# Two attention stages in a six-stage kernel: retention's scores six slots later, and softmax scores made twice

## The chip, the cores and the metric

The kernel runs on one core of one Trainium2 chip. The metric is the device time of one execution in microseconds (us); lower is better. A core has a matrix engine (TensorE, PE in the profile), three engines for element-wise work (VectorE or DVE, ScalarE or ACT, GpSimd or POOL), an engine that only issues transfers here (SyncE, SP) and 16 DMA engines. Each engine runs its own instructions in order; semaphores tie them together. TensorE writes to PSUM, which has eight banks of 512 float32 columns; the others work from SBUF or PSUM.

## What is computed

Sixteen sequences x of 256 tokens and 128 channels go through two layers, each a feed-forward net, an attention and another net. Two attentions matter here, both with 16 heads of 8 channels. The first is retention, with no softmax:

```python
qkv = x @ w_qkv.T                       # q, k are rotated and scaled, position by position
scores = jnp.einsum('bhtd,bhsd->bhts', q, k) * HEAD_DIM ** (-0.5)
scores = scores * mask[None]            # causal, decaying
y = jnp.einsum('bhts,bhsd->bhtd', scores, v)    # then group norm, gate, projection
```

The second is plain attention:

```python
q = q * scale
attn = jax.nn.softmax(jnp.einsum('bnhd,bmhd->bhnm', q, k), axis=-1)
out = jnp.einsum('bhnm,bmhd->bnhd', attn, v)
return out.reshape(B, N, C) @ w_proj.T + b_proj
```

## The kernel before

`program` runs six stages one after the other on an x that stays in SBUF: routed net, `retention`, routed net, `relative_ffn` (attention with relative positions and a mixture), `plain_attention`, `relative_ffn`. The change touches the second and the fifth.

In both a batch is one sequence. Its q and k are made in float32, split into three bfloat16 parts whose sum is the float32 value (`parts`), written by SP to DRAM in six combinations (`write_slots` in retention, `stack_parts` in the other: six DMAs, 768 KB) and read back as `qs` and `ks` (two DMAs of 384 KB), where a head's combinations lie on 48 partitions (the tiles have 96, the rest zero). So one bfloat16 matmul over 96 rows gives scores of nearly float32 precision. The loads of batch i overwrite those of batch i-2, so SP waits for the scores of that batch.

Retention is written as slots. A step has NS = 16 slots n; `at(s, n, slot)` gives the batch i for which slot number `slot`, counted from the start of its own first step, falls on slot n of step s, or None. Each engine goes through steps and slots and issues whatever is due, so the numbers set the order on each engine. For batch i: x is normalised and turned (slot 6), q and k projected (9, 11), v (13), the gate g (15); the parts are made in slots 17 to 21; scores of group r (four heads) and half follow at 36 + 4r + 2half, masks one slot later on DVE, the copies of the other block on ACT (`later`), values at 42 + 4r; then statistics (56), group means on PE (58, 62), 64 to 69 the scale, shift and gate, 72 the output projection, 74 the addition to x. Scores go to three banks (`sd`) and one (`so`), y to two, and all small products share two banks (`desk`, a `Bench`), taken in the order of the list `order`: an item waits until the one two places before it has been taken away.

Plain attention runs `softmax_attention` with `rel` false. In each step of 16 iterations n, PE makes the scores of two heads and one half of the queries (`scores`, 128 queries x 256 keys, twice; four banks `sr`), DVE takes their maximum over the keys (`maxima`, L1849), ACT the exponential with that maximum as bias and the sum as a by-product (`exponentials`, L1718: 32 of 256 columns a batch, each with a read of the accumulator), PE transposes the result in four blocks (`turn_round`, L1586: 64 a batch), ACT and DVE copy the blocks to SBUF in turn (`take_turned`, L1698 and L1688: 8 each), and PE multiplies them with the values (`values`, L1599). The sums are inverted, spread and transposed, and multiply y. Three steps overlap: projections of batch s, parts of s-1, attention of s-2, the end of s-3.

## Time and profile before

| | us |
|---|---|
| time, median of 3 runs (range) | 3241.97 (3240.16 to 3244.74) |
| the profiled execution | 3240.78 |
| its span, first to last instruction | 3239.0 |
| PE / PE weight loads busy | 2893.4 / 2344.7 |
| DVE / ACT / POOL busy | 2067.5 / 1993.3 / 1996.2 |
| retention | about 320 to 580 |
| plain attention | about 1883 to 2238 |

A matmul's duration includes the latency of its end, and an ACT duration overlaps with that of the one before it, so in this kernel the distance from start to start tells what an instruction costs its engine. A row that ends in x4 is four instructions merged. The granted clock is a share of TensorE's full speed of 2.4 GHz; half is 1.2 GHz. A bracket at the end of a row is the time in which the engine was idle before it, and what ended that.

### The profile page before, as it was taken

The page shows a single profiled execution, that of the slowest core. Times are in us where ns is not written, and L with a number is a line of the kernel's source. Part 1 is how long each engine was busy: PE and PEld are TensorE (multiplying, and loading weights), DVE is VectorE, ACT ScalarE, POOL GpSimd, SP SyncE. Part 2 cuts the span into 40 slices and gives each one's busy share as a digit, 9 for nine tenths or more (in the row PEclk, how much of TensorE's full clock was granted, in tenths as well). Part 3 has the DMA queues.
Part 4 walks back from the last instruction along what each step waited for, and adds up shares of the span by engine and source line. Part 5 has one row for each costly group of instructions (what it writes and reads, how often), then busy time and mean ns, then how long its engine had stood idle before and what let it go on. Part 6 is the DMA issues. An engine that isn't in the chain of part 4 may idle for free. (4 is left out here: it accounts for less than half of the span.)

```text
span 3239.0 us, 64162 instructions
## 1 busy us (share of the span) xinstructions
PE 2893.4 (89%) x21536; PEld 2344.7 (72%) x21536; DVE 2067.5 (64%) x4642; ACT 1993.3 (62%) x5893; POOL 1996.2 (62%) x2415
## 2 busy tenths in 40 slices
PE   6999677699969999997999979896999999979998
PEld 4788555488857877785788856664777778858886
DVE  5444466454458888885555558885788888745554
ACT  2232333223258988985444459996899889844443
POOL 4223554322268878874999932222788778669997
PEclk8999889899979999998999989998999999989999
DMA  3000445000022212212545533332122112145544
GB/s 106 1 1 1 110 109 111 1 1 1 1 48 56 45 40 45 55 41 107 193 186 195 186 88 79 79 79 49 41 49 52 41 41 58 23 177 190 193 186 170
DMA packets 145535, 261.88 MB, mean 81 GB/s; under 512 B 13402, under 2 KB 118106, under 8 KB 122298
## 3 DMA queue, kind: packets, MB, share of 16 engines
q1 hardware_dynamic: 145210, 257.78, 27.3%
q8 instruction: 176, 2.88, 0.4%
q14 instruction: 149, 1.22, 0.1%
HBM read 204.06 MB, written 53.67 MB: 80 GB/s over the span
## 5 line engine op out<-in xcount | busy, mean ns | idle before, releaser
L2252 POOL TENSOR_TENSOR f6m_ht_lo<-f6m_ht,f6m_ht_hi 128x512 fp32r<-128x512 f32 x256 | 331.1, 1311 | 32.3 <-ACT f6m_ht_hi L2197 23.3
L2252 POOL TENSOR_TENSOR f4m_ht_lo<-f4m_ht,f4m_ht_hi 128x512 fp32r<-128x512 f32 x256 | 331.9, 1316 | 30.4 <-ACT f4m_ht_hi L2197 22.2
L2232 DVE SCALAR_TENSOR_TENSOR f4m_ht<-f4m_hr,f4m_gate 128x512 f32<-128x512 f32 x256 | 176.4, 691 | 167.4 <-PE f4m_hr L2128 159.3
L2232 DVE SCALAR_TENSOR_TENSOR f6m_ht<-f6m_hr,f6m_gate 128x512 f32<-128x512 f32 x256 | 176.3, 691 | 167.1 <-PE f6m_hr L2128 160.5
L2197 ACT ACTIVATE f6m_ht_hi<-f6m_ht 128x512 fp32r<-128x512 f32 x256 | 161.9, 634 | 190.6 <-DVE f6m_ht L2232 190.5
L2197 ACT ACTIVATE f4m_ht_hi<-f4m_ht 128x512 fp32r<-128x512 f32 x256 | 161.9, 634 | 189.9 <-DVE f4m_ht L2232 189.6
L1718 ACT ACTIVATE f6a_pr<-f6a_sr,f6a_nm 128x256 f32<-128x256 f32 x512 | 241.4, 487 | 47.9 <-DVE f6a_nm L1849 47.8
L1718 ACT ACTIVATE f4a_pr<-f4a_sr,f4a_nm 128x256 f32<-128x256 f32 x512 | 241.2, 487 | 47.9 <-DVE f4a_nm L1849 47.9
L1718 ACT ACTIVATE a_pr<-a_sr,a_nm 128x256 f32<-128x256 f32 x512 | 257.9, 585 | 11.2 <-DVE a_nm L1849 11.1
L1980 POOL TENSOR_TENSOR f4a_rr<-f4a_tmp 128x256 f32<-128x256 f32 x256 | 187.7, 733 | 101.9 <-DVE f4a_tmp L1857 100.0
L1980 POOL TENSOR_TENSOR f6a_rr<-f6a_tmp 128x256 f32<-128x256 f32 x256 | 187.5, 732 | 101.7 <-DVE f6a_tmp L1857 99.6
L1857 DVE TENSOR_TENSOR f4a_tmp<-f4a_ur,f4a_turn 128x512 f32<-128x512 f32 x256 | 174.9, 683 | 76.7 <-PE f4a_ur L1558 73.2
L1857 DVE TENSOR_TENSOR f6a_tmp<-f6a_ur,f6a_turn 128x512 f32<-128x512 f32 x256 | 174.9, 684 | 76.1 <-PE f6a_ur L1558 72.6
L1849 DVE TENSOR_REDUCE a_nm<-a_sr 128x2 f32<-128x512 f32 x256 | 173.4, 684 | 57.5 <-PE a_sr L1570 57.5
L1849 DVE TENSOR_REDUCE f4a_nm<-f4a_sr 128x2 f32<-128x512 f32 x256 | 175.9, 687 | 41.4 <-PE f4a_sr L1576 41.1
L1849 DVE TENSOR_REDUCE f6a_nm<-f6a_sr 128x2 f32<-128x512 f32 x256 | 175.8, 687 | 41.4 <-PE f6a_sr L1576 41.0
L1986 POOL TENSOR_TENSOR f6a_rr_lo<-f6a_rr,f6a_rr_hi 128x256 fp32r<-128x256 f32 x256 | 190.6, 745 | 0.9 <-ACT f6a_rr_hi L1792 0.9
L1986 POOL TENSOR_TENSOR f4a_rr_lo<-f4a_rr,f4a_rr_hi 128x256 fp32r<-128x256 f32 x256 | 190.2, 743 | 0.9 <-ACT f4a_rr_hi L1792 0.9
L1574 PE MATMUL f6a_sr<-f6a_pe_hi,f6a_rr_hi 128*128 128x256 f32 x512 | 187.3, 366 | 0.0
L1574 PE MATMUL f4a_sr<-f4a_pe_hi,f4a_rr_hi 128*128 128x256 f32 x512 | 187.3, 366 | 0.0
L1586 PE MATMUL a_tr<-all_table,a_pr 128*128 128x128 f32 x1024 | 157.4, 276 | 5.8 <-ACT a_pts L1698 3.4
L1718 ACT ACTIVATION_READ_ACCUMULATOR a_pr<-a_sr,a_nm 128x1 f32 x512 | 162.3, 317 | 0.0
(420 smaller groups left out, 9783.9 us busy)
## 6 DMA issues: line engine op xcount, KB each, us to landing
f4m_gate<-f4m_gates SPq DMA_DIRECT2D x64, 1024.0 KB, 4.6
f6m_gate<-f6m_gates SPq DMA_DIRECT2D x64, 1024.0 KB, 4.6
r_scratch<-r_parts SPq DMA_DIRECT2D x32, 192.0 KB, 2.2
all_qs<-r_scratch SPq DMA_DIRECT2D x16, 384.0 KB, 4.8
all_ks<-r_scratch SPq DMA_DIRECT2D x16, 384.0 KB, 6.7
f4a_scratch<-f4a_parts SPq DMA_DIRECT2D x32, 192.0 KB, 2.2
all_qs<-f4a_scratch SPq DMA_DIRECT2D x16, 384.0 KB, 5.2
all_ks<-f4a_scratch SPq DMA_DIRECT2D x16, 384.0 KB, 6.6
```

The costliest lines, as they stand in the source:

```text
L1574: nc.tensor.matmul(out, rr_hi[at], pe_hi[:, :], start=False, stop=False)
L1586: mm = nc.tensor.transpose(ring.bank(b, n // 2)[:, o:o + P], pr[:, n % 4, x, st * P:(st + 1) * P], k.ident)
L1718: last = nc.scalar.activation(pr[:, n % 4, x, :], sr.bank(b, n)[:, x * T:(x + 1) * T], ACT.Exp, bias=nm[:, n % SB, x:x + 1], accum_out=zs[ ...
L1849: nc.vector.tensor_reduce(nm[:, n % SB, :], sr.bank(b, n).rearrange("p (x s) -> p x s", x=2), AX.X, ALU.max, negate=True).then_inc(nm_read ...
L1857: nc.vector.tensor_tensor(tmp[:, hs % 2, :, :], ur.bank(b, hs).rearrange("p (u t) -> p u t", u=2), turn[:, :, :], ALU.mult).then_inc(ur.em ...
L1980: nc.gpsimd.tensor_tensor(rr[:, hs % RAW, :], tmp[:, hs % 2, 0, :], tmp[:, hs % 2, 1, :], ALU.add)\
L1986: nc.gpsimd.tensor_tensor(rr_lo[:, hs % RRS, :], rr[:, hs % RAW, :], rr_hi[:, hs % RRS, :], ALU.subtract)\
L2197: nc.scalar.activation(ht_hi[:, n % RB, :], ht[:, n % RB, :], ACT.Copy).then_inc(hi_ready, 1)
L2232: nc.vector.scalar_tensor_tensor(ht[:, n % RB, :], hr[:, n % HB, :], 0.0, gate[:, q % GB, n % LOADED, :], ALU.max, ALU.mult).then_inc(ht_r ...
L2252: nc.gpsimd.tensor_tensor(ht_lo[:, n % RB, :], ht[:, n % RB, :], ht_hi[:, n % RB, :], ALU.subtract)\
```

## The change

In retention all slots from the scores on are six higher (scores 42 + 4r + 2half, values 48 + 4r, statistics 62, and so on to 80), the stage has one more step, and the desk's order is another: gm, gv, xt, q, k, v, o, g instead of xt, o, q, gm, k, v, gv, g.

Plain attention gets a function of its own, in the manner of retention. The scores are made twice. First by queries, as before, in two banks instead of four; only DVE reads them, for the maxima. POOL splits the negated maxima of a half of the heads into three bfloat16 parts (`split_maxima`, six operations), PE transposes them (slots 43 and 51), ACT copies 24 rows to `mrow` and SP copies those to rows 96 to 119 of that batch's `qs` (`move`: 24 rows to eight heads). Rows 96 to 119 of the keys hold a one where a row belongs to the head (`pick_rows`, once). Then PE makes the scores by keys over 120 rows (`turned`, slots 50 to 65, three banks), which gives the transposed scores less the maximum; ACT takes the exponential of 512 columns straight into `pts`, without bias or sum; values follow at 56 + 4r. Columns of ones in the values' tile give the sums in the same product; y goes to all 512 columns of its bank, is transposed (71), divided on DVE (`divide`, 72), transposed back (74) and projected (77). The normalisation of x moves from DVE to POOL, one cast of q and k from DVE to ACT. There are three buffers for qs and ks instead of two, and four for the values instead of two, both cleared at the start of the stage.

```diff
+KROWS = ROWS + 3 * H // 2
...
-    LAST = B + 3
+    LAST = B + 4
...
-            order += [(name, s - lag) for name, lag in (("xt", 0), ("o", 4), ("q", 0), ("gm", 3), ("k", 0), ("v", 0), ("gv", 3),
+            order += [(name, s - lag) for name, lag in (("gm", 4), ("gv", 4), ("xt", 0), ("q", 0), ("k", 0), ("v", 0), ("o", 4),
...
-                i = at(s, n, 4 * NS + 8)
+                i = at(s, n, 4 * NS + 14)
...
-                i = at(s, n, 3 * NS + 10)
+                i = at(s, n, 4 * NS)
...
-                i = at(s, n, 3 * NS + 14)
+                i = at(s, n, 4 * NS + 4)
...
-                            i = at(s, n, 36 + 4 * r + 2 * half)
+                            i = at(s, n, 42 + 4 * r + 2 * half)
...
-                        i = at(s, n, 42 + 4 * r)
+                        i = at(s, n, 48 + 4 * r)
...
-    softmax_attention(nc, tag, x_sb, k, io)
...
+    NS, NB, VB, SB, PB = 16, 3, 4, 2, 3
+    SCORES, TURNED = 2 * NS, 3 * NS + 2
+    HALF = H // 2
+    TOP = 3 * HALF
+    MOVED = 16
...
+            order += [(name, s - lag) for name, lag in (("m1", 3), ("xt", 0), ("v", 0), ("yt", 4), ("qk", 0), ("yb", 4), ("m0", 2),
+                                                       ("o", 4)) if 0 <= s - lag < B]
...
+            def move(i, half):
+
+                desk.done(sp, f"m{half}", i)
+                if i:
+                    sp.wait_ge(moved[half], i * MOVED)
+                sp.dma_start(queries(i)[ROWS:KROWS, half * HALF:(half + 1) * HALF, :],
+                             mrow[0:TOP, half, :].unsqueeze(1).to_broadcast([TOP, HALF, T])).then_inc(moved[half], 16)
+
+            for s in range(B + 3):
+                if 0 <= s - 3 < B:
+                    move(s - 3, 1)
+                if 0 <= s - 2 < B:
+                    move(s - 2, 0)
+                if s < B:
+                    if s >= 1:
+                        sp.wait_ge(stacked, s * LANDED)
+                    sp.wait_ge(parts_ready, s + 1)
+                    write_slots(sp, parts[:, s % 2], scratch[s % 2], bounced)
+                    if s == 2:
+                        sp.wait_ge(third_clear, 4)
+                    if s >= NB:
+                        sp.wait_ge(st_filled, (s - NB + 1) * NS)
+                    sp.wait_ge(bounced, (s + 1) * BOUNCED)
+                    for u, dst in enumerate((queries(s), keys(s))):
+                        sp.dma_start(dst[0:USED, :, :].rearrange("s h t -> s (h t)"),
+                                     scratch[s % 2, u].rearrange("n (d h) t -> (n d) (h t)", h=H)).then_inc(stacked, 16)
...
+            def scores(i, n):
+                r, jj, t = n // QUAD, n // 2 % 2, n % 2
+                g = i * NS + n
+                if n == 0:
+                    pe.wait_ge(stacked, (i + 1) * LANDED)
+                if g >= SB:
+                    pe.wait_ge(nm_ready, g - SB + 1)
+                for x in range(2):
+                    h = QUAD * r + 2 * jj + x
+                    mm = nc.tensor.matmul(sr[:, g % SB, x * T:(x + 1) * T], queries(i)[0:ROWS, h, t * P:(t + 1) * P],
+                                          keys(i)[0:ROWS, h, :], start=True, stop=True)
+                mm.then_inc(sr_filled, 1)
+
+            def turned(i, m):
+                r, jj, t = m // QUAD, m // 2 % 2, m % 2
+                g = i * NS + m
+                if g == 0:
+                    pe.wait_ge(ones_set, 6)
+                if m % (NS // 2) == 0:
+                    pe.wait_ge(moved[m * 2 // NS], (i + 1) * MOVED)
+                if g >= PB:
+                    pe.wait_ge(pr_ready, g - PB + 1)
+                for x in range(2):
+                    h = QUAD * r + 2 * jj + x
+                    mm = nc.tensor.matmul(st[:, g % PB, x * T:(x + 1) * T], keys(i)[0:KROWS, h, t * P:(t + 1) * P],
+                                          queries(i)[0:KROWS, h, :], start=True, stop=True)
+                mm.then_inc(st_filled, 1)
+
+            def values(i, r):
+                if r == 0:
+                    desk.done(pe, "v", i)
+                    if i:
+                        pe.wait_ge(y_copied, i)
+                pe.wait_ge(pr_ready, i * NS + (r + 1) * QUAD)
+                for t in range(TT):
+                    for j in range(QUAD):
+                        q = slice(j * QUAD * HD, (j + 1) * QUAD * HD)
+                        mm = nc.tensor.matmul(y_ps[q, r // 2 * T:(r // 2 + 1) * T], vm[:, i % VB, t, r, q], pts[:, r % 2, t, j, :],
+                                              start=(r == 0 and t == 0), stop=(r == QUAD - 1 and t == TT - 1),
+                                              skip_group_check=True)
+                mm.then_inc(av_done, 1)
...
+                for half in range(2):
+                    i = at(s, n, SCORES + 11 + half * 8)
+                    if i is not None:
+                        name = f"m{half}"
+                        pe.wait_ge(split, (2 * i + half) * 6 + 6)
+                        desk.free(pe, name, i)
+                        for t in range(TT):
+                            mm = nc.tensor.transpose(desk.bank(name, i)[:, t * P:(t + 1) * P], mf[:, half, t, :], k.ident)
+                        mm.then_inc(desk.filled, 1)
...
+                i = at(s, n, 4)
...
+                i = at(s, n, 6)
...
+                i = at(s, n, TURNED + 21)
...
+                i = at(s, n, 8)
...
+                i = at(s, n, TURNED + 24)
...
+                i = at(s, n, TURNED + 27)
...
+            pe.wait_ge(k.loaded, k.loaded_count)
+            for s in range(LAST + 1):
+                for n in range(NS):
+                    i = batch(s, 2)
+                    if i is not None:
+                        scores(i, n)
+                    project(s, n)
+                    for m in range(NS):
+                        i = at(s, n, TURNED + m)
+                        if i is not None:
+                            turned(i, m)
+                    for r in range(QUAD):
+                        i = at(s, n, TURNED + 6 + 4 * r)
+                        if i is not None:
+                            values(i, r)
...
+            def exponentials(i, m):
+                r, jj, t = m // QUAD, m // 2 % 2, m % 2
+                g, R = i * NS + m, i * QUAD + r
+                act.wait_ge(st_filled, g + 1)
+                if m % QUAD == 0 and R >= 2:
+                    act.wait_ge(av_done, R - 1)
+                nc.scalar.activation(pts[:, r % 2, t, 2 * jj:2 * jj + 2, :].rearrange("p x t -> p (x t)"), st[:, g % PB, :],
+                                     ACT.Exp).then_inc(pr_ready, 1)
...
+            def pick_rows():
+
+                act.wait_ge(loaded, LOADS)
+                for n, tile in enumerate((k.ks[ROWS:KROWS, 0, :, :], k.ks[ROWS:KROWS, 1, :, :], k3[ROWS:KROWS, :, :])):
+                    for half in range(2):
+                        copy(tile[:, half * HALF:(half + 1) * HALF, :],
+                             pick[ROWS:KROWS, :].unsqueeze(2).to_broadcast([TOP, HALF, T])).then_inc(ones_set, 1)
...
+                    copy(parts[:, i % 2, 0, :, :], desk.bank("qk", i).rearrange("p (u t) -> p u t", u=2))
+                    copy(qk[:, :, :].rearrange("p u t -> p (u t)"), desk.bank("qk", i)).then_inc(desk_taken, 1)
+                    if i == 1:
+                        pick_rows()
...
+            def maxima(i, n):
+                r, jj, t = n // QUAD, n // 2 % 2, n % 2
+                g, q = i * NS + n, 2 * i + r // 2
+                dve.wait_ge(sr_filled, g + 1)
+                if n % (NS // 2) == 0 and q >= 2:
+                    dve.wait_ge(split, (q - 2) * 6 + 3)
+                at_ = r % 2 * QUAD + 2 * jj
+                nc.vector.tensor_reduce(nm[:, r // 2, t, at_:at_ + 2], sr[:, g % SB, :].rearrange("p (x s) -> p x s", x=2), AX.X,
+                                        ALU.max, negate=True).then_inc(nm_ready, 1)
...
+            def divide(i):
+                desk.full(dve, "yt", i)
+                if i:
+                    desk.full(dve, "yb", i - 1)
+                bank = desk.bank("yt", i).rearrange("p (h g c) -> p h g c", h=2, c=QUAD * HD)
+                for hf in range(2):
+                    last = nc.vector.reciprocal(rz[:, hf, :, :], bank[:, hf, :, 16 * (1 - hf):16 * (1 - hf) + 2])
+                last.then_inc(rz_ready, 1)
+                dve.wait_ge(rz_ready, i + 1)
+                for hf in range(2):
+                    last = nc.vector.tensor_tensor(
+                        yn[:, :, :].rearrange("p t (j c) -> p (t j) c", c=QUAD * HD)[:, :, 16 * hf:16 * hf + 16]
+                        .rearrange("p g (r d) -> p g r d", d=HD),
+                        bank[:, hf, :, 16 * hf:16 * hf + 16].rearrange("p g (r d) -> p g r d", d=HD),
+                        rz[:, hf, :, :].unsqueeze(3).to_broadcast([P, 2 * QUAD, 2, HD]), ALU.mult)
+                last.then_inc(yn_ready, 1)
...
+            def clear_third():
+                for tile in (q3, k3):
+                    for rows in (slice(32, 64), slice(64, ROWS)):
+                        nc.vector.memset(tile[rows, :, :].rearrange("p s t -> p (s t)").bitcast(F32), 0.0).then_inc(third_clear, 1)
...
+                    nc.vector.tensor_copy(parts[:, i % 2, 1, :, :], rest[:, :, :]).then_inc(part1, 1)
+                    if i == 1:
+                        clear_third()
...
+            def split_maxima(i, half):
+
+                q = 2 * i + half
+                pool.wait_ge(nm_ready, i * NS + (half + 1) * (NS // 2))
+                if i:
+                    desk.full(pool, f"m{half}", i - 1)
+                whole = nm[:, half, :, :]
+                first, second, third = (mf[:, half, :, n * HALF:(n + 1) * HALF] for n in range(3))
+                nc.gpsimd.tensor_copy(b1[:, :, :], whole).then_inc(split, 1)
+                pool.wait_ge(split, q * 6 + 1)
+                nc.gpsimd.tensor_tensor(r1[:, :, :], whole, b1[:, :, :], ALU.subtract).then_inc(split, 1)
+                pool.wait_ge(split, q * 6 + 2)
+                nc.gpsimd.tensor_tensor(first, whole, r1[:, :, :], ALU.subtract).then_inc(split, 1)
+                nc.gpsimd.tensor_copy(b2[:, :, :], r1[:, :, :]).then_inc(split, 1)
+                pool.wait_ge(split, q * 6 + 4)
+                nc.gpsimd.tensor_tensor(third, r1[:, :, :], b2[:, :, :], ALU.subtract).then_inc(split, 1)
+                pool.wait_ge(split, q * 6 + 5)
+                nc.gpsimd.tensor_tensor(second, r1[:, :, :], third, ALU.subtract).then_inc(split, 1)
...
+                    i = at(s, n, SCORES + 9 + half * 8)
...
-    k.qs, k.ks = a.sb("qs", [ROWS, 2, H, T], BF16), a.sb("ks", [ROWS, 2, H, T], BF16)
+    k.qs, k.ks = a.sb("qs", [KROWS, 2, H, T], BF16), a.sb("ks", [KROWS, 2, H, T], BF16)
```

## Rows read from the trace of the kernel before

**Rows 1.** Busy time of each engine, two stages: us, busy (instructions), granted clock, DMA.

```profile
320.00:582.00 262.00, 191.71 (x2201) 143.12 (x2200) 155.07 (x380) 90.12 (x225) 129.48 (x180) 0.87 0.46 102
...
1883.00:2238.00 355.00, 303.15 (x2816) 221.51 (x2816) 282.90 (x578) 325.25 (x1248) 74.40 (x96) 0.96 0.34 73
```

**Rows 2.** The same view, a steady stretch of plain attention.

```profile
1942.00:1962.00 20.00, 18.16 (x176) 13.37 (x175) 17.04 (x36) 19.80 (x79) 4.65 (x6) 1.00 0.37 81
```

**Rows 3.** Timeline of ScalarE, plain attention: start, duration, engine, line, names.

```profile
1940.70 0.61 ACT L1718 ACTIVATE a_pr<-a_sr,a_nm 128x256 f32<-128x256 f32 x1
...
1941.15 0.52 ACT L1698 ACTIVATE a_xt<-a_desk 128x256 f32<-128x256 f32 x1
1941.41 0.62 ACT L1718 ACTIVATE a_pr<-a_sr,a_nm 128x256 f32<-128x256 f32 x1
...
1942.31 0.76 ACT L1698 ACTIVATE a_pts<-a_tr 128x512 f32<-128x512 f32 x1
1942.79 0.65 ACT L1718 ACTIVATE a_pr<-a_sr,a_nm 128x256 f32<-128x256 f32 x1
```

**Rows 4.** Timeline of SyncE's queue, retention: first write of batches 1, 8, 9, 15.

```profile
350.84 0.38 SPq L889 DMA_DIRECT2D r_scratch<-r_parts  x1
...
453.50 0.38 SPq L889 DMA_DIRECT2D r_scratch<-r_parts  x1
...
457.88 0.32 SPq L1022 DMA_DIRECT2D all_qs<-r_scratch  x1
...
465.27 0.38 SPq L889 DMA_DIRECT2D r_scratch<-r_parts  x1
...
550.39 0.38 SPq L889 DMA_DIRECT2D r_scratch<-r_parts  x1
```

**Rows 5.** Timeline of TensorE, retention; idle time before a row in brackets.

```profile
464.88 0.61 PE L1037 MATMUL r_sd<-all_qs,all_ks 96*128 96x128 bf16 x4 [2.71 <-DMA all_ks<-r_scratch]
...
485.13 1.13 PE L1107 MATMUL r_desk<-r_xt,r_w 128*128 128x256 f32 x4 [0.57 <-DVE r_qp L1279]
```

**Rows 6.** Busy time by engine, the stretch of that wait.

```profile
458.00:471.00 13.00, 9.77 (x99) 7.18 (x98) 7.33 (x19) 5.13 (x13) 6.62 (x10) 0.74 0.56 132
```

**Rows 7.** Timeline of TensorE, plain attention.

```profile
1941.72 1.13 PE L1638 MATMUL a_desk<-a_xt,a_wq 128*128 128x256 f32 x4 [0.16 <-ACT a_xt L1698]
1942.69 0.39 PE L1570 MATMUL a_sr<-all_ks,all_qs 96*128 96x256 bf16 x2
1942.91 0.60 PE L1586 MATMUL a_tr<-all_table,a_pr 128*128 128x128 f32 x4
1943.35 0.39 PE L1570 MATMUL a_sr<-all_ks,all_qs 96*128 96x256 bf16 x2
...
1944.10 1.07 PE L1599 MATMUL a_y<-a_pts,a_vm 128*32 128x256 f32 x16
1945.10 0.39 PE L1570 MATMUL a_sr<-all_ks,all_qs 96*128 96x256 bf16 x2
...
1947.47 0.44 PE L1610 MATMUL a_desk<-all_table,a_rz 128*128 128x128 f32 x2 [0.87 <-DVE a_rz L1894]
```

**Rows 8.** Timeline of VectorE, plain attention.

```profile
1943.11 0.69 DVE L1849 TENSOR_REDUCE a_nm<-a_sr 128x2 f32<-128x512 f32 x1 [0.72 <-PE a_sr L1570]
1943.72 0.68 DVE L1688 COPY a_pts<-a_tr 128x512 f32<-128x512 f32 x1
```

**Rows 9.** Groups by line, GpSimd in plain attention: count, busy us, mean ns, idle before.

```profile
L1999 POOL TENSOR_TENSOR a_rest<-a_qk,a_parts 128x512 f32<-128x512 f32 x16 | 18.6, 1163 | 169.9 <-DVE a_parts L1920 169.9
...
L1967 POOL TENSOR_TENSOR a_veps<-a_mv,all_half 128x2 f32<-128x2 f32 x16 | 3.1, 197 | 9.5 <-DVE a_mv L1825 9.5
```

**Rows 10.** Timeline of all engines at plain attention's beginning and end.

```profile
1887.33 1.76 DVE L1841 MEMSET a_vm<- 128x2048 f32 x1 [0.38 <-issue]
...
1904.60 1.65 PE L1570 MATMUL a_sr<-all_ks,all_qs 96*128 96x256 bf16 x7 [6.61 <-issue]
...
2236.80 0.72 POOL L2015 TENSOR_TENSOR all_x<-all_x,a_ob 128x256 f32<-128x256 f32 x1
```

More of the change, by code:

```diff
@@ L1046, in scores @@
                     h = j * QUAD + r
-                    mm = nc.tensor.matmul(so[:, j, :], ks[:, par, h, 0:P], qs[:, par, h, P:T], start=True, stop=True)
+                    mm = nc.tensor.matmul(so[:, j, :], ks[0:ROWS, par, h, 0:P], qs[0:ROWS, par, h, P:T], start=True, stop=True)
                 mm.then_inc(so_filled, 1)
@@ L1557, in relate @@
                 for u in range(2):
-                    mm = nc.tensor.matmul(out[:, u * T:(u + 1) * T], w.ws[:, u, h, :], qs[:, b[1], h, :],
+                    mm = nc.tensor.matmul(out[:, u * T:(u + 1) * T], w.ws[:, u, h, :], qs[0:ROWS, b[1], h, :],
                                           start=True, stop=True)
```

291 lines of the change are left out of this document (274 added, 17 removed).

## Prediction

> **What bounds the kernel now.** I read the busy time by stage first [rows 1]. The change touches two stages: retention (320 to 582 us) and plain attention (1883 to 2238 us). In plain attention TensorE (PE) is busy 303 of 355 us and ScalarE (ACT) 325. In one steady window of 20 us [rows 2] ACT is busy 19.8 us at a full TensorE clock, so ACT sets the pace. One batch is what a stretch of this length holds.
>
> The ACT timeline [rows 3] prices its work by start to start, since busy times overlap: an exponential of 256 columns with its accumulator read takes 0.45 us, a copy of 256 columns 0.26, one of 512 columns 0.48. A batch has 32 exponentials (14.4), 8 copies of turned probabilities (3.8) and small copies (xt, ob and rzb 0.26 each, qk 0.48, vm 0.31, together 1.6): 19.8 us.
>
> Retention is another case: all its engines are idle for a good part [rows 1]. SyncE writes a batch's parts at 350.84 (batch 1) and 550.39 (batch 15) [rows 4], so 199.55 us for 14 batches, 14.25 us each. The distances alternate, near 11.8 us (453.50 to 465.27) and near 17 us. PE says why: at 464.88 it starts the scores after 2.7 us of waiting for the stacked keys [rows 5]. From the first write to that start is 11.4 us. The clock granted in that stretch is 0.74 [rows 6], and the 96-row matmuls there take 0.61 us for four against 0.40 at full clock. In a batch after a stall the loads had a head start, and none is waited for: hence the alternation.
>
> **Retention, part by part.** No instruction is added. The scores of batch i go from slot 36 to slot 42 (16 slots a step), and everything behind them (mask, copies, values, group norm, output) by six as well, so those distances stay. The parts of a batch are written at slot 21 and its loads land 11.4 us later; the scores' place, counted in slots, moves 6 of 16 of a step away, 4.4 us of an 11.8 us step. The wait is 2.7 us here (4.4 in another batch, with another clock state), so it is covered. SP's wait before it overwrites the buffers (scores of batch i-2, now ending at slot 8 of the step instead of 2) stands behind the parts' writes, which end later than that: nothing. What is late next: the step without a load wait is 11.8 us. In it PE waits 0.57 us for VectorE (DVE) to take q [rows 5], and about 0.5 more for k; the new order of the desk's two banks puts a long-empty bank ahead of k, but makes v wait for q and the output for k. Going down the slots with the prices of plain attention's PE and DVE [rows 7, 8] (PE: 12 groups of scores at 0.22, values four times 0.8, q and k 0.97 each, v, output and g half of that each, transposes and group means 0.8, together 10.1; DVE 9.3), the chain POOL rstd, ga, nb, two masks, gated, qp, mask, kp, output, g closes in 11.0 us. I take 11.0, between 10.3 (PE's work alone) and 12.5 (DMA pace, below). Batch 0's scores still wait some 2 us for the first loads, so batch 2's write comes 13.2 behind batch 1's, at 364; 13 steps of 11.0 later batch 15's at 507, against 550.4. Behind it lie the same loads and the same tail. Retention gives 43 us; at 12.5 a step 24, at 10.3 52.
>
> **Plain attention, part by part.** Per batch in us, start to start:
> ACT loses the 32 exponentials, their accumulator reads and its 8 turned copies, and gains 16 exponentials of 512 columns. No row shows one: the copy of 512 is 0.48, twice the old pair is 0.90; with no accumulator and no per-row bias it is nearest to the copy. 16 x 0.48 = 7.7, and 3.0 of copies (five of 256, y and two qk of 512, v): 10.7. With 0.90 it would be 17.4.
> PE keeps 16 score pairs (0.22 each, 1942.69 to 1942.91 [rows 7]) and values (four groups at 1.00, 1944.10 to 1945.10), loses 64 transposes (four in 0.44), and gains 16 pairs of transposed scores over 120 rows. Sum: 32 x 0.22 = 7.0; values 4.0; qk 0.97; v and the output projection half of that each, 1.0; 12 transposes 1.3: 14.3, against 17 before. The 120 rows against 96 are not in the trace: between nothing and the ratio of rows (0.05 a pair, 0.9 a step); the rows with 128 and 96 rows differ in type too, so they don't decide, and I take nothing. The Trainium skill (TensorE: Matmul & The Clock Gate, section Step-by-step: what each phase is for) says that loading time goes with columns and that the row count doesn't matter; by that the addition is 0, by the ratio the step would be 15.9.
> DVE keeps 16 maxima at 0.61 [rows 8], loses 8 copies: 9.7, and 2.0 of division, cast and statistics: 11.7.
> GpSimd (POOL) keeps two operations of 1.16 us [rows 9] and two additions, takes the normalisation from DVE (1.6) and gets 12 small dependent operations on 16 columns. The nearest row is the one on two columns, 0.20 busy [rows 9], with 0.08 to hand over: 3.4, total about 10; at 1.16 each, the row on 512 columns, it would be 20, and POOL the bound, but 16 columns are near to two.
>
> So PE becomes the bound at 14.3. **What it waits for.** The scores' ring falls from four banks to two. DVE starts a maximum 0.42 us after the pair starts (1942.69 to 1943.11) and is done 0.69 later, so PE can fill every 0.61 us, while a light slot has only 0.44 us of PE work. Going down the sixteen slots, the heavy ones (values, qk) absorb this; the run of light slots behind each adds 0.6 to 0.7 in all. The maxima's split for the second half (1.7 us on POOL, behind the output's additions) ends at about the time that PE gets to its transposes: nothing, 0.7 if POOL's operations are slower. Step: 15.0.
> **The new DMA.** SP's queue gets two copies a batch (24 rows to eight heads, 96 KB). The first half goes ahead of the parts' writes and has four slots to land. The second is behind the stacking of qs and ks. From the start of the qk matmul: parts ready at 5.6 us (latency of PE, ACT 0.96, POOL 1.16 twice, DVE 0.43 and hand-overs), loads issued 4.38 later, at 10.0 (453.50 to 457.88 [rows 4]), keys landed 7.0 after that (to 464.88 [rows 5]), the copy behind them at 18.2 if its 96 KB take an eighth of the loads' 768, 0.9, and a little for landing; the bounds are nothing, and the 4.4 of the whole group of writes. It is needed at the matmuls of slot 10 of the next step, one step plus 3.1 us after the same start: 15.0 + 3.1 = 18.1. It just fits. Each microsecond that it is later costs half a microsecond a step, because a late step gives the next one room.
>
> **Ends of the stage.** Filling is longer: DVE clears 4096 columns instead of 2048 before it scales wq (1.76 us for 2048 [rows 10]), and in step 1 it clears four blocks of that size (7.1) while ACT writes six blocks of 2048 columns (10.7, at 0.85 ns a column from the two copies of [rows 3]). Scores, now at 1904.6 [rows 10], are ready at 1906, but the first maximum comes at about 1912 and step 2, short of transposed work, ends at 1923.5. Step 3 is 14.5, then 14 steps of 15.0: the last scores end at 2148. The tail is longer, as the last batch goes through maxima, split, transposes, DMA, exponentials, values, division, output: 17.5 against 10. The stage ends at 2165.5 instead of 2237.5 [rows 10]: 72 us.
>
> **Sum.** The profiled execution took 3240.78 us (span 3239.0), 1.2 under the median of the three. 3240.8 - 43 - 72 = 3125.8, on the median's footing 3127. Retention's bounds move it by -9 and +19, plain attention's (14.5 or 16.5 a step) by -7 and +21.
>
> **Rivals.**
> 1. The second copy comes late. With a wait of 2.7 us, as retention's, the clock falls too, as it does after such a wait [rows 6]. Step about 19, so 14 x 4 more: 3183. For it: the copy fits with no margin, and its rows are 512 bytes into only 24 partitions. Against: half of each delay is given back.
> 2. Retention is paced by DMA: its writes (4.4 us to the loads' issue) and loads (7.0) use the same queue and 11.4 is more than my 11.0, so writes queue behind the loads: 12.5 a step, 3146. Against: a write needs the engines only from a microsecond after its issue, and the DMA share is about a half in this stage.
> 3. ACT isn't relieved: an exponential of 512 columns costs the same 0.90 as two pairs. Step 17.4: 3161. Retention without any gain would be 3170; these are the cases in which a half of the change does nothing.
> 4. Slower: PE's many short waits on the ring of two let the clock fall to 1.2 GHz for all of plain attention. PE's 14.3 us are then near 29 a step, 14 x 14 more: 3323. It decides from 115/14 = 8.2 us a step, that is if over half of PE's work runs at the lower level. Against: in that window PE waits several times (0.87 us at 1947.47 [rows 7]) at clock 1.00 [rows 2], and is busier per step after the change. The Trainium skill (the same page, section A second HAM failure mode: psum-queue depth-cycling) describes such short idles between groups as PE cycles through PSUM banks, with the clock going up and down; by that rule this rival holds in part, by the rows it doesn't.
>
> **Chances.** Forecast 3127: 0.62 (own range 3105 to 3155, with rival 2's 0.10 near its upper end). Rival 1: 0.13. Rival 3: 0.06. Rival 4: 0.03. Faster than 3105: 0.05. A remaining 0.01 is for no gain. The range goes to 3185; it leaves out 0.05 below and about 0.1 above. A difference of 0.2%, 6.5 us, is what can be told from no change: faster 0.95, same 0.01, slower 0.04.
>
> **What the profile would show.** Retention: writes evenly 11 us apart, no wait for ks in the steady part, clock 1.00. Wrong if waits for ks return at slot 42. Plain attention: PE about 95% busy, ACT about 70%, exponentials 0.48 apart, PE waiting for maxima by 0.1 to 0.2 in light slots, writes 15 us apart. Wrong if PE waits for the copied maxima at the ninth transposed pair, or if ACT is still full.

## The result, and the profile after

The kernel with the change takes 3151.43 us (median of 4 runs, 3148.44 to 3152.39) beside 3241.3 for the kernel before on the same chip: a ratio of 0.9719, with a 95% interval of 0.9703 to 0.9736. It is 90 us faster; 115 were forecast, and 3151 lies in the range of 3105 to 3185.

The profiled execution has a span of 3149.7 us against 3239.0. By stage: retention's last addition to x comes at 540.85 instead of 577.53 (36.7 us gained, 43 forecast), before and then after:

```profile
577.53 0.72 POOL L1357 TENSOR_TENSOR all_x<-all_x,r_ob 128x256 f32<-128x256 f32 x1 [3.35 <-ACT r_ob L1147]
```

```profile
540.85 0.72 POOL L1358 TENSOR_TENSOR all_x<-all_x,r_ob 128x256 f32<-128x256 f32 x1 [3.35 <-ACT r_ob L1148]
```

The plain attention's stage, from its load of wq to that of the next stage, takes 301.7 instead of 355.7 us (54.0, forecast 72). The other stages together are 1.4 us longer. Between kernels with the same code such a stretch varies by more than that: the one from retention's end to plain attention's load of wq takes 1303 to 1310 us in the profiles of this case, and this attention stage 301.7 to 303.8 us in the four profiles that have its code unchanged. So a single profile tells a stage to about 2 us, and of those four this one is the shortest.

Busy time by stretch in the profile after: the stretch, then busy us (instructions) of PE, PEld, DVE, ACT and POOL, the granted clock, the DMA share and GB/s. The first two rows answer to [rows 1], the last to [rows 2]; the third is one steady step of retention.

```profile
320.00:547.00 227.00, 184.99 (x2206) 139.94 (x2205) 155.44 (x385) 91.39 (x225) 131.97 (x180) 0.89 0.53 117
1848.00:2150.00 302.00, 256.28 (x2432) 166.69 (x2432) 202.81 (x425) 200.03 (x422) 138.20 (x320) 0.92 0.47 96
441.00:452.00 11.00, 10.22 (x136) 7.72 (x133) 9.43 (x23) 5.61 (x14) 7.70 (x12) 1.00 0.68 145
1957.00:1973.00 16.00, 15.17 (x156) 10.16 (x152) 11.90 (x26) 11.68 (x26) 8.64 (x21) 1.00 0.54 112
```

The last row shows what was forecast in kind: ACT is relieved (11.68 of 16 us, where it had 19.8 of 20), PE is busy 95%, the clock is full. But the stretch that holds one batch is 16.0 us long, not 15.0.

In retention the steady step, from one batch's first write to the next one's, is what the prediction put at 11.0. SyncE's queue, after: the first write of batches 2 and 15, which answers to [rows 4].

```profile
363.98 0.38 SPq L890 DMA_DIRECT2D r_scratch<-r_parts  x1
...
508.56 0.38 SPq L890 DMA_DIRECT2D r_scratch<-r_parts  x1
```

364 was forecast for the first and 507 for the second; the last eleven steps are 11.25 us each to within 0.01. TensorE in that stretch, after (idle time ahead of a row in brackets, with what ended it), for [rows 5]:

```profile
449.54 0.39 PE L1038 MATMUL r_sd<-all_qs,all_ks 96*128 96x128 bf16 x4
450.70 0.38 PE L1122 MATMUL r_desk<-r_qv,r_group 128*128 128x1 f32 x2 [0.78 <-DVE r_qv L1289]
451.01 0.64 PE L1061 MATMUL r_y<-r_att,r_vm 128*32 128x256 f32 x8
```

The steady wait of 2.7 to 4.4 us for keys is gone, four score matmuls take 0.39 and not 0.61, and what is left is a wait of 0.78 us for VectorE, once a step, in a place that the prediction didn't name.

GpSimd in plain attention, after, one period:

```profile
1957.55 0.19 POOL L1844 CAST a_b<-a_nm 128x16 bf16<-128x16 f32 x1
...
1958.86 0.22 POOL L1853 TENSOR_TENSOR a_mf<-a_r,a_mf 128x16 f32<-128x16 f32 x1
...
1966.05 1.16 POOL L1865 TENSOR_TENSOR a_rest<-a_qk,a_parts 128x512 f32<-128x512 f32 x1 [0.61 <-ACT a_qk L1658]
1968.14 1.17 POOL L1870 TENSOR_TENSOR a_parts<-a_rest,a_parts 128x512 bf16<-128x512 f32 x1 [0.93 <-DVE a_parts L1800]
1969.42 0.20 POOL L1826 TENSOR_TENSOR a_veps<-a_mv,all_half 128x2 f32<-128x2 f32 x1
...
1970.52 1.58 POOL L1833 TENSOR_SCALAR a_xn<-all_x,a_mv,a_rstd 128x128 f32<-128x128 f32 x2
1972.07 0.73 POOL L1880 TENSOR_TENSOR a_ob<-a_ob,a_bp 128x256 f32<-128x256 f32 x1
1972.87 0.72 POOL L1883 TENSOR_TENSOR all_x<-all_x,a_ob 128x256 f32<-128x256 f32 x1
1973.54 0.20 POOL L1844 CAST a_b<-a_nm 128x16 bf16<-128x16 f32 x1
```

From the parts on POOL never stands still: second product, statistics, normalisation, bias, x, and behind them the split of the maxima's second half. TensorE, after, in the same step:

```profile
1958.26 0.39 PE L1540 MATMUL a_sr<-a_k,a_q 96*128 96x256 bf16 x2
1959.14 0.44 PE L1581 MATMUL a_desk<-all_table,a_mf 128*128 128x128 f32 x2 [0.49 <-POOL a_mf L1853]
```

PE waits for that split, and the q and k for which POOL waits 7 us later stand behind it on PE. That closes a ring, a chain of waits that goes out from one engine, through another and back to the first: from the split's end at 1959.08 to the product at 1966.05 it is 6.97 us, then POOL's operations, start to start, 2.09, 1.28, 1.10, 1.55, 0.80 and 0.67, and the split itself 1.54: 16.00.

### The profile page after: what moved, and what is told of

The parts are those of the page before. It is cut to its first block and busy times, and to the rows that moved or that the text cites. A ratio compares the mean times of both kernels' runs of the same rounds, so it can differ in the third digit from the quotient of the medians.

```text
span 3149.7 us, 62295 instructions
## 1 busy us (share of the span) xinstructions
PE 2841.9 (90%) x21152; PEld 2288.3 (73%) x21152; DVE 1985.9 (63%) x4489; ACT 1867.4 (59%) x5067; POOL 2059.4 (65%) x2639
## 3 DMA queue, kind: packets, MB, share of 16 engines
q14 instruction: 141, 1.16, 0.1%
## 5 line engine op out<-in xcount | busy, mean ns | idle before, releaser
L2707 POOL TENSOR_TENSOR f4m_ht_lo<-f4m_ht,f4m_ht_hi 128x512 fp32r<-128x512 f32 x256 | 330.4, 1310 | 33.5 <-ACT f4m_ht_hi L2652 24.2
L1760 DVE TENSOR_REDUCE a_nm<-a_sr 128x2 f32<-128x512 f32 x256 | 166.6, 685 | 60.4 <-PE a_sr L1540 59.5
L1666 ACT ACTIVATE a_pts<-a_st 128x512 f32<-128x512 f32 x256 | 141.6, 598 | 28.3 <-PE a_st L1555 27.1
L2025 PE MATMUL f6a_sr<-all_ks,all_qs 96*128 96x256 bf16 x512 | 143.2, 280 | 12.9 <-ACT f6a_pr L2173 10.0
L2025 PE MATMUL f4a_sr<-all_ks,all_qs 96*128 96x256 bf16 x512 | 143.5, 280 | 12.0 <-ACT f4a_pr L2173 9.9
```

Source lines behind the costliest of these rows:

```text
L1666: nc.scalar.activation(pts[:, r % 2, t, 2 * jj:2 * jj + 2, :].rearrange("p x t -> p (x t)"), st[:, g % PB, :], ACT.Exp).then_inc(pr_ready, 1)
L1760: nc.vector.tensor_reduce(nm[:, r // 2, t, at_:at_ + 2], sr[:, g % SB, :].rearrange("p (x s) -> p x s", x=2), AX.X, ALU.max, negate=True). ...
L2025: mm = nc.tensor.matmul(out, qs[0:ROWS, b[1], h, t * P:(t + 1) * P], ks[0:ROWS, b[1], h, :], start=True, stop=not rel)
L2707: nc.gpsimd.tensor_tensor(ht_lo[:, n % RB, :], ht[:, n % RB, :], ht_hi[:, n % RB, :], ALU.subtract)\
```

## The experiments

Stage times below are taken as above, from profiles; "step" is the distance of the additions to x in plain attention and of the first writes in retention. An interval of a ratio is 5 us wide to either side, so most single edits to the changed kernel overlap with it by the whole time (0.9703 to 0.9736); what each does is read from steps and waits in its trace.

**Each half alone.** The kernel before with the new retention:

```diff
-                            i = at(s, n, 36 + 4 * r + 2 * half)
+                            i = at(s, n, 42 + 4 * r + 2 * half)
...
```

(and the other slots of that function and its desk order with it; plain attention stays.)

> Only retention's half of the change. Theory: its stage ends 37 us earlier, as in the whole change, with 11.25 us between the writes of two batches, and the other stages keep their length: 3204 us. Rival: some of that is given back or gained by the stages behind it (the relative attention began 37.0 us earlier but plain attention only 34.5): then the time is 3207 or more, and the difference stands again between those two stages' starts.

Measured: 3199.11 us, ratio 0.9878 (0.9863 to 0.9893), 38 us gained. The kernel before with the new plain attention:

```diff
-    softmax_attention(nc, tag, x_sb, k, io)
+    NS, NB, VB, SB, PB = 16, 3, 4, 2, 3
...
```

> Only plain attention's half; retention as before. Theory: the stage takes 302 us instead of 356, 54 less, with 16.0 us a batch: 3187 us. Rival: the halves are not independent (the stages share buffers for q and k): then the two gains don't add up to 90 us.

Measured: 3187.26 us, ratio 0.9841 (0.9824 to 0.9857), 50 us gained, with the same step of 16.0. 38 and 50 make 88, and the whole change 90: within the intervals the halves add up, and each can be studied by itself. With the first half alone retention ends 39.9 us earlier than before, not 36.7, though its code is that of the whole change; the part on its end below says why.

**What sets the attention's step.** The two additions of a batch go behind the next split on POOL:

```diff
-    LAST = B + 3
+    LAST = B + 4
...
-                i = at(s, n, TURNED + 29)
+                i = at(s, n, TURNED + 36)
```

> After the change, plain attention's two additions on GpSimd (bias, x) go from slot TURNED+29 to TURNED+36, behind the split of the second half of the maxima instead of ahead of it. Theory: the step of 16.0 us is a loop through GpSimd's queue (split, TensorE's transposes, qk, rest, parts, normalisation, bias, x, split); the additions are 1.5 us of it, so TensorE's wait of 0.5 to 0.7 us for a_mf goes and the step falls to about 15.3, which is TensorE's work with its waits for two banks: 14 x 0.7 = 10 us less than after, 3141. Rival: the ring of two banks or the last DMA sets the step: then it stays at 16.0 and the wait turns up in another row.

Measured: 3143.29 us, ratio 0.9707 (0.9692 to 0.9721). Of the steps in the middle most are 15.3 us, a few 15.6 or 16.0; the stage takes 296.2 instead of 301.7. No operation was made shorter, so it was POOL's order and not its load. PE's wait for the split is gone from the steady steps. The other suspect was the ring of two score banks:

```diff
-    NS, NB, VB, SB, PB = 16, 3, 4, 2, 3
+    NS, NB, VB, SB, PB = 16, 3, 4, 3, 2
```

> After the change, plain attention's scores by queries in three banks instead of two, those by keys in two instead of three. Theory of GpSimd's loop: the waits for a_nm go (0.2 to 0.4 us at a time), but the step stays at 16.0 and the time within 2 us of 3151. Rival, as forecast: TensorE with the ring of two banks sets the step, then it falls by 0.6 to 0.8 us to 15.3, 3141. Two banks for the other ring may cost: then TensorE waits for a_pts and the step is longer than 16.0.

Measured: 3149.09 us, ratio 0.9726 (0.9711 to 0.974). The step is 16.16, no shorter, and PE's wait for the split grew from 0.49 to 0.84, so a bank more for these scores, taken from the keys' scores, only moves the wait. This kernel, TensorE:

```profile
1952.93 0.44 PE L1581 MATMUL a_desk<-all_table,a_mf 128*128 128x128 f32 x2 [0.84 <-POOL a_mf L1853]
```

Both edits together:

> The bias and x additions stand behind the next split on GpSimd, and the queries' scores have three banks, the keys' two. Theory (with the split moved, GpSimd's loop of 16.0 us is broken, and what is left over TensorE's own 14.6 to 15.0 us are waits for a bank of the ring): the step falls from the 15.3 us of the late bias alone to 15.0 or 15.1, the attention's stage from 296.1 to about 293, and the whole to about 3139. Rival (the 15.3 us are TensorE's own work with what lies between two kinds of matmul, and banks only move the waits; the keys' probabilities then lose what the maxima gain): the step stays at 15.3 or rises to 15.45, as three banks alone added 0.16, stage 296 to 300, whole 3141 to 3146.

Measured: 3138.63 us, ratio 0.9687 (0.9672 to 0.9701). Eight of the first eleven steps are 15.10 us (the others 15.2, 15.3 and 16.0), but the stage is 295.8, hardly better than 296.2: its end is longer, and with two banks for the keys' scores PE waits 2.9 us in all for the exponentials, against 0.3. A steady step of this kernel, columns as above:

```profile
1964.00:1979.10 15.10, 15.02 (x154) 10.13 (x152) 11.75 (x27) 11.66 (x27) 8.64 (x21) 1.00 0.57 119
```

PE is busy all of it. So the third bank is worth 0.2 us a step once POOL's ring is open, net of what the keys' scores lose by theirs, and nothing before. The odd 16 us steps of both kernels have a wait like this one (late additions alone, TensorE):

```profile
2074.01 0.39 PE L1555 MATMUL a_st<-a_q,a_k 120*128 120x256 bf16 x2 [0.61 <-DMA a_q<-a_mrow]
```

That is rival 1's copy. The wait is there in some steps of the 16.0 us kernel too (0.3 to 0.4 us, four times), and doesn't lengthen them. In all these kernels it comes at times, by 0.2 to 1.6 us, and the granted clock stays at 1.00 in the 8 us behind the longest three.

**The fill.** The four clears behind batch 1's norm, not ahead of it:

```diff
-                    if i == 1:
-                        clear_third()
                 i = at(s, n, -NS + 12)
                 if i is not None:
                     measure(i)
+                    if i == 1:
+                        clear_third()
```

> As after, but VectorE clears the third pair of key and query buffers behind batch 1's norm and not ahead of it. Theory (the fill of the attention is late because these four clears, 1.76 us each and 0.48 apart, hold VectorE from 1870.5 to 1879.0 while batch 0's maxima wait behind them): the first maximum comes 4 to 7 us earlier after the stage's start (24.5 to 27.5 instead of 31.5), TensorE's wait of 7.3 us for it is gone, the stage takes 295 to 298 instead of 301.7, the whole about 3146. Rival (the start is paced by ScalarE's build of the pick rows, which ends 11 us behind the start of VectorE's clears, or by TensorE itself): the first maximum moves by under 1 us or what it gains is lost again before batch 0 is written, stage 301 to 302, whole 3151.

Measured: 3142.55 us, ratio 0.9701 (0.9686 to 0.9715). VectorE, first after, then with the early clears:

```profile
1877.27 1.76 DVE L1791 MEMSET a_k<- 32x2048 f32 x1 [0.48 <-issue]
...
1879.76 2.65 DVE L1760 TENSOR_REDUCE a_nm<-a_sr 128x2 f32<-128x512 f32 x4
```

```profile
1863.39 1.76 DVE L1791 MEMSET a_k<- 32x2048 f32 x1 [0.48 <-issue]
...
1868.96 1.29 DVE L1760 TENSOR_REDUCE a_nm<-a_sr 128x2 f32<-128x512 f32 x2 [1.96 <-PE a_sr L1540]
```

Counted from the stages' starts (1848.3 and 1844.5), the first maximum moves from 31.5 to 24.4 us, 7 us, and the stage falls from 301.7 to 297.6. Of the 7 us 3 are lost before the first addition to x, which comes 4.1 earlier (72.5 instead of 76.6); what takes them wasn't tried apart. The ratio gives 6 us and not 4, which is within its interval; in this profile the end of retention is 4.0 us shorter too, though its code is the same. The next experiment bears on that.

**The end of retention.** 28 transposes of a constant keep PE busy where it waits for the last batch's keys:

```diff
                 if r == 0 and half == 0:
+                    if i == B - 1:
+                        for _ in range(28):
+                            nc.tensor.transpose(y_ps[:, 0, T:T + P], k.ident, k.ident)
                     pe.wait_ge(stacked, (i + 1) * LANDED)
```

> As after, with 28 extra transposes of a constant on TensorE ahead of its wait for the last batch's stacked keys, into a bank that is overwritten behind them. Nothing is left out. Theory (the end of retention is 5 us longer than before because TensorE stands still 3.1 us and then works at half the clock, 0.61 us where the same group took 0.40): the granted clock stays at full, retention ends 3 to 5 us earlier, the whole 3147. Rival (the end is long because more of the batch's work now lies behind its last transfer, whatever the clock): the clock stays up but the end moves by under 1.5 us, or later by the extra work, the whole 3150 to 3153.

Measured: 3144.89 us, ratio 0.9706 (0.9689 to 0.9722). The transposes went into the bank in which batch 14's sums are still running and spoil those, so, against what was expected of it, this kernel does leave out part of that batch's sums; no time hangs on it. TensorE's first scores of the last batch, before and then after:

```profile
561.94 0.40 PE L1037 MATMUL r_sd<-all_qs,all_ks 96*128 96x128 bf16 x4 [0.92 <-DMA all_ks<-r_scratch]
```

```profile
520.15 0.61 PE L1038 MATMUL r_sd<-all_qs,all_ks 96*128 96x128 bf16 x4 [3.11 <-DMA all_ks<-r_scratch]
```

The 12 us from there, before, after, and with the extra transposes (columns as above):

```profile
562.00:574.00 12.00, 9.37 (x144) 6.84 (x144) 8.35 (x22) 4.08 (x11) 2.76 (x6) 0.98 0.01 1
```

```profile
520.00:532.00 12.00, 11.85 (x108) 8.68 (x112) 6.28 (x16) 2.90 (x7) 1.48 (x3) 0.50 0.00 1
```

```profile
517.60:529.60 12.00, 9.34 (x145) 6.80 (x143) 8.34 (x22) 4.08 (x11) 2.79 (x6) 1.00 0.01 3
```

From batch 15's write to the last addition it takes 32.3 us after, 27.1 before and 27.1 with PE kept busy. Most of that distance is the same in all three: the scores start 11.5 or 11.6 us behind the write. The difference lies behind the scores, and there every kernel of this case falls in line by its clock:

| kernel | PE's wait ahead of the scores, us | granted clock in the 12 us from there | scores to last addition, us |
|---|---|---|---|
| before; plain attention's half alone | 0.9; none | 0.98; 1.00 | 15.6; 15.6 |
| extra transposes (alone; both kernels with all edits) | none | 1.00; 1.00; 0.94 | 15.6; 15.6; 15.8 |
| early clears | 2.7 | 0.86 | 17.1 |
| three banks | 4.6 | 0.82 | 17.6 |
| late additions with three banks; retention's half alone | 3.1; 3.2 | 0.73; 0.73 | 18.7; 18.8 |
| after; mean first | 3.1; 3.3 | 0.50; 0.50 | 20.7; 20.7 |
| late additions | 3.1 | 0.50 | 20.8 |

So it is the clock that this end hangs on, by up to 5.1 us. What the wait's length does not tell is how far the clock falls: 3.1 us stand ahead of 0.50 and of 0.73, and why isn't shown. The six kernels with the same code for retention end 28.3 to 32.4 us behind the write, so one profile of a kernel can't tell the change's effect on this end better than to 4 us.

**Retention's step.** ScalarE copies the mean ahead of its first part, not behind it:

```diff
+                i = at(s, n, 4 * NS + 1)         # mean, five lines
+                ...
                 i = at(s, n, NS + 1)             # first part
...
-                i = at(s, n, 4 * NS + 1)
-                ...
```

> As after, but in retention ScalarE copies the mean of a batch ahead of its part of the values' scaling, not behind it. Theory (the 11.25 us of a retention step are set by TensorE's wait of 0.78 us for the scaled queries, and those wait on VectorE for the mean that ScalarE copies late): the mean comes some 0.5 us earlier, the step falls to 10.7 to 10.9 us, thirteen steps give 5 to 7 us, the whole 3145 with an unchanged attention. Rival (the step is set by a loop through GpSimd, or the copy that now comes later is waited for instead): the step stays between 11.2 and 11.4, the whole 3150 to 3152.

Measured: 3142.78 us, ratio 0.9701 (0.9686 to 0.9715). The wait for `r_qv` is gone from the steady steps. The copy's delay that was expected as the reason is the smaller part (0.41 us of VectorE's wait for `r_mean`); the larger part, 1.00 us, is in the subtraction behind it, and this edit removes both. VectorE and GpSimd after:

```profile
449.24 1.15 DVE L1285 TENSOR_TENSOR r_dmean<-r_ymv,r_mean 128x1 f32<-128x1 f32 x1 [0.41 <-ACT r_mean L1148]
450.43 0.22 DVE L1289 SCALAR_TENSOR_TENSOR r_qv<-r_dmean,r_ymv 128x1 f32<-128x1 f32 x1
```

```profile
449.23 1.15 POOL L1345 TENSOR_TENSOR r_rest<-r_qk,r_parts 128x512 f32<-128x512 f32 x1 [0.55 <-ACT r_parts L1148]
```

With the mean first, VectorE, GpSimd and then TensorE:

```profile
411.10 0.15 DVE L1285 TENSOR_TENSOR r_dmean<-r_ymv,r_mean 128x1 f32<-128x1 f32 x1
```

```profile
411.63 1.16 POOL L1345 TENSOR_TENSOR r_rest<-r_qk,r_parts 128x512 f32<-128x512 f32 x1 [0.61 <-ACT r_parts L1148]
```

```profile
417.54 0.40 PE L1038 MATMUL r_sd<-all_qs,all_ks 96*128 96x128 bf16 x4 [1.46 <-DMA all_ks<-r_scratch]
```

A subtraction of one column takes 1.15 us where it starts 0.01 behind a GpSimd operation of 1.15 us, and 0.15 where it starts ahead of it. In the first case both end within 0.01 us of each other: VectorE stood still until GpSimd was done. The change itself made them meet: in the kernel before, the first 13 of the 16 such subtractions take 0.15 to 0.17 us, after 1.15 or 1.16, and with retention's half alone 1.15. Before, VectorE:

```profile
415.59 0.15 DVE L1284 TENSOR_TENSOR r_dmean<-r_ymv,r_mean 128x1 f32<-128x1 f32 x1
```

The Trainium skill (SBUF — State Buffer, section SBUF: two separate sides) says that these two engines share a pair of ports as an exclusive lock, and that an operation of VectorE with two inputs in SBUF waits for the whole of a GpSimd operation that reads SBUF and was first. The rows agree. With the microsecond gone the steps are 10.4 us at their shortest, but the waits for keys return (13.9 us in the stage against 6.2), and from batch 3's write to batch 15's it is 131.3 us, 10.94 a step, against 135.1 (11.26).

**All that helped, together.** Late additions, early clears, the mean first, and the 28 transposes behind a wait for batch 13's output in the half of the bank pair that no running sum uses; then the same with three and two banks:

```diff
-                            nc.tensor.transpose(y_ps[:, 0, T:T + P], k.ident, k.ident)
+                            nc.tensor.transpose(y_ps[:, 1, T:T + P], k.ident, k.ident)
```

> As after, with four edits together: the attention's bias and x additions behind the next split, the four clears behind batch 1's norm, the mean copied first in retention, and 28 extra transposes ahead of the wait for the last batch's stacked keys, now into a part of the bank that no running sum uses. If the parts add up as measured singly (attention stage 5.6 and 4.0 us, retention step 3.8 us, end of retention 5.2 us where the profiled run of after had the clock at half): retention's last x addition 26 to 28 us behind batch 15's write, attention's stage 292 us, the whole 3130 to 3136, some 17 us under after. Rival (they overlap: the shorter fill and the later additions both give back the same wait): attention's stage 296, the whole 3137 to 3142.

> As all_23, with three banks for the queries' scores and two for the keys'. The late bias with three banks had a step of 15.10 us against 15.3 but a longer end. If only the step counts: 2 us under all_23. If the end gives it back again, as it did without the other edits (stage 295.8 against 296.1): within 1 us of all_23.

Measured: 3138.28 us, ratio 0.9684 (0.9671 to 0.9697), and 3140.10 us, ratio 0.969 (0.9677 to 0.9703). In the first the attention's stage is 292.8, where the single gains foretell 292.1: there they add up. That the two edits give back the same wait, the rival, is out for that stage, though the whole lands in the rival's range (3137 to 3142) and above the 3130 to 3136 of the theory. The reason is retention, where the gains don't add up: from batch 2's write to the last addition it is 172.0 and 170.9 us in these two, and 171.4 with the extra transposes alone. The clock at the end is kept (table above), but the last batch's scores start 14.4 and 12.5 us behind its write, not 11.5, where 26 to 28 us in all were expected and 30.0 and 28.2 came. And the steps from batch 3's write to batch 15's take 132.4 and 133.1 us, against 131.3 with the mean first alone: in both one step takes 14 us, behind a wait for keys of about 2 us. With two and three banks, TensorE and the 12 us from there:

```profile
417.39 0.61 PE L1042 MATMUL r_sd<-all_qs,all_ks 96*128 96x128 bf16 x4 [2.06 <-DMA all_ks<-r_scratch]
```

```profile
417.00:429.00 12.00, 11.61 (x135) 8.94 (x136) 7.77 (x21) 4.93 (x13) 5.75 (x9) 0.86 0.56 115
```

So once the step is short enough for keys to be waited for, a wait can cost clock in the middle of the stage too; how much of the 14 us is the clock wasn't tried apart. By the ratios these kernels are 11 and 9 us faster than after, and not told apart from each other or from late additions with three banks (0.9687).

## Why the prediction was right or wrong

**Direction and bounds: right.** The loads bounded retention, ACT bounded plain attention, and both bounds went. The misses are 6 us in retention and 18 in plain attention; together 24 of the 115, both to the same side, so nothing cancelled. Both steps lie within the bounds that were set for them (11.25 in 10.3 to 12.5, 16.0 in 14.5 to 16.5), and 3151 lies in the range for that reason. But neither was set by what the forecast named, and that they fell inside is in part luck.

**Retention's step, 11.0 forecast, 11.25 measured.** The load's cover was right (no steady wait for keys), the chain named was not the one that closed. The step waits for the mean, by way of a subtraction held behind GpSimd. It had been priced as a small operation, which it was before (0.15 us); six slots later it lies beside a big one of GpSimd and takes 1.15. Batch 15's write came 1.6 us later than forecast. Without that wait a step is 10.4, PE's own work (bound 10.3), and then the chain of write and load, 11.4 us before [rows 4, 5], shows again: PE waits for keys in 11 places of the stage, and the average step is 10.94. That is rival 2's chain, at a smaller price.

**"Behind it lie the same loads and the same tail": wrong, 5.2 us here.** From batch 15's write to its scores it is alike, 11.6 and 11.5 us. But PE now waits 3.1 us ahead of those scores, where it waited 0.9, and the 12 us behind them are granted 0.50 of the clock, where they had 0.98; so the rest takes 20.7 us and not 15.6. With PE kept busy it is 15.6 again. In the other five profiles of the same code this part takes 17.1 to 20.8, so 5.2 is near the most of what the change costs here.

**The exponential of 512 columns, 0.48 of 0.48 to 0.90: right.** Where nothing lies between them they start 0.48 to 0.52 apart, and ACT is busy 11.68 us a step. Rival 3 is out.

**120 rows cost nothing: right.** TensorE, after:

```profile
1957.31 0.38 PE L1555 MATMUL a_st<-all_qs,all_ks 120*128 120x256 bf16 x2
1957.53 0.38 PE L1540 MATMUL a_sr<-a_k,a_q 96*128 96x256 bf16 x2
1957.75 0.38 PE L1555 MATMUL a_st<-all_qs,all_ks 120*128 120x256 bf16 x2
...
1960.07 0.38 PE L1555 MATMUL a_st<-all_qs,all_ks 120*128 120x256 bf16 x2
1960.39 1.07 PE L1568 MATMUL a_y<-a_pts,a_vm 128*32 128x256 f32 x16
1961.39 0.39 PE L1540 MATMUL a_sr<-a_k,a_q 96*128 96x256 bf16 x2
```

A pair over 120 rows is followed after 0.22 us, as one over 96 rows is. The rule of the Trainium skill cited in the forecast holds.

**PE's own work, 14.3 forecast:** near 15.0. In the step of 15.10 with three banks it waits for hardly anything that the trace names. What was left out are small gaps, among them about 0.1 ahead of each of the four groups of values: 0.32 from 1960.07 to 1960.39 above, where pairs stand 0.22 apart. The rest of the 0.7 wasn't told apart.

**The ring of two, 0.6 to 0.7: mis-sized,** 0.2 once nothing else is late (15.3 against 15.1, where the keys' scores gave up a bank for it).

**"Ends at about the time that PE gets to its transposes: nothing, 0.7 if POOL's operations are slower": the step of the forecast that failed most.** The operations were priced right (0.28 apart; 1.54 the split, 1.7 forecast). What failed is to compare two times of one step, and not to follow the ring: PE's transposes wait for the split, q and k stand behind those on PE, and POOL's next split stands behind its work on q and k. That sum is 16.0, though POOL itself is busy for only 8.6 of it; without the two additions (0.80 and 0.67) it would be 14.5, an estimate from the rows above, which is less than PE needs. Eleven steps at 1.0 over the forecast are 11 us (from the x transposes of batch 4 to those of batch 15 it is 176.0). With the three shorter steps at the end the 14 steps behind batch 1's scores took 220 us and not 210: 10 of the 18. Moving two additions of 0.8 took 0.7 a step and 5.5 in the stage.

**The fill: 4.6 us of the 18.** ACT's blocks were priced right (7.3 and 3.7 us for six). A clear's row is 1.76 us long, as forecast, but clears start 2.24 apart. The forecast for the first maximum was 29.2 us behind the stage's start and it came at 31.5, most of it because each of the four clears has 0.48 us of idle time ahead of it, 1.9 in all: the forecast had priced them by their rows and not start to start. From there to batch 0's last maximum it took 13.8 us and not 11.5 (45.3 against 40.7). The clock was low there for longer than before: the stage's third 16 us had 0.61 of it and the fourth 0.93, where before the third had 1.00 (1915 to 1931). What that cost wasn't tried. The fill at three places, after:

```profile
1880.00:1896.00 16.00, 12.06 (x48) 6.18 (x49) 12.45 (x25) 2.29 (x6) 9.61 (x22) 0.61 0.30 69
1896.00:1912.00 16.00, 15.24 (x138) 10.41 (x136) 12.27 (x24) 12.14 (x26) 7.24 (x18) 0.93 0.60 121
1912.00:1928.00 16.00, 15.25 (x154) 10.20 (x153) 12.03 (x27) 11.79 (x27) 8.64 (x20) 1.00 0.57 120
```

The first maximum at 24.4 with the clears moved shows that these clears had a free place 10 us earlier. The remaining 3.7 us lie in the stage's end, behind the last scores (21.2 us where 17.5 were forecast); it wasn't taken apart.

**Rival 1** was right that the second copy has no margin: at 15.0 to 15.3 us a step it is late now and then, by up to 1.3 us, and a step is lengthened. At 16.0 the odd wait of 0.3 to 0.4 costs the step nothing. **Rival 4** is out: in each step PE waits 0.49 us for the split and 0.21 for a bank of the ring of two, and the clock is 1.00 in all steady stretches. The rule of the Trainium skill named there, that such short idles make the clock go up and down, didn't hold for waits of that length here.

## What to carry to other kernels

Where an engine does work of two batches in one fixed order, add up each ring that goes out of it and comes back in the same step; busy shares (POOL 54%, PE 95%) don't show it, and a step that repeats to 0.01 us does. Then move the operation that nobody waits for behind the one that somebody does. After operations have been moved, look again at the small ones that stand beside a big one of another engine. And once the waits of a loop are gone, look at the last iteration: a wait is still there and may cost more than its length.

## What was not expected of the hardware

An operation of VectorE on one column took 1.15 us beside a GpSimd operation and 0.15 without (in each of the first 13 steps of after, and of the kernel with the mean first). A wait of 3.1 us for a transfer at the end of retention was followed by 12 us at a granted clock of 0.50 in two kernels and of 0.73 in a third, and with it the same work took 15.6 us at full clock and up to 20.8.
